# Output projection of a linear-attention layer as seven half products with features on the partitions

## The chip, the cores and the metric

One of the eight cores of a Trainium2 chip runs the whole program. The metric is the device time of one execution in microseconds. TensorE (PE) multiplies, VectorE (DVE), ScalarE (ACT) and GpSimd (POOL) work element by element, SyncE (SP) issues the loads and stores.

## What is computed

```python
qkv = silu(x @ qkv_w.T)                # 1024 tokens (4 batches of 256), 32 heads of 128 features
attn = linear_attention(q, k, v)       # decayed, causal, per head and batch
normed = norm_w * attn * rsqrt(mean(attn ** 2) + eps)    # over all 4096 features of a token
y = sigmoid(x @ gate_w.T) * normed
x = layernorm(x + y @ out_w.T)         # the output projection, 4096 -> 512
...                                    # then base projection, router, LoRA experts, a second layernorm
```

Everything is float32. Each factor of a product is split into a high part, rounded by the copy, and a low part, the rest, and a product takes three matmuls: high by high, high by low, low by high.

## The kernel before

The 32 heads are done in eight groups of four. The work of a group is a fixed order of stages, written out by hand for each engine; semaphores tie the queues together. The stages of group g are QK0 (q and k of the group's first head), V0 and V1 (the values of its four heads, half of the tokens each), the output stage for the group before, G01 (gates of two heads), QK1, G23, QK2, QK3. Attention and score matmuls of single heads stand between the products. The output stage of the last group is part of the tail.

**Projections in seven products.** A stage such as G01 multiplies a 2 by 2 arrangement of weight blocks by a 2 by 2 arrangement of token halves with seven products in place of eight (the Winograd form of Strassen's method). The sums of the token blocks are made once. Those of the weights are made per load: `sums` on GpSimd (L1737) makes four further blocks out of four loaded ones, in three instructions (L1742 with 512 columns, L1745 and L1749 with 256). ScalarE copies the high parts (`sums_hi`, L389), VectorE subtracts them for the low parts (`sums_lo`, L1031), in two parts: A has units 0 to 2, for products 1, 5 and 6, B has units 3 to 6, for products 2, 7, 3 and 4. The high and low parts live in a ring of 16 units. The full blocks are in two staging buffers, so that a load waits for the splits of the load two before it. TensorE runs p1, p4 of the stage before, p5, p6, p2, p7, p3 (L1976 and after); between them ScalarE copies banks (`u2_copy`, `p5_copy`, `u3_copy`) and VectorE adds (`c22_add`, `c12_add`), which p4 and the next stage's copies wait for.

**The output stage.** The weight rows of the four heads come in two loads, oa and ob (`rows_load`), and go to the ring as they are; ScalarE scales them by norm_w on the way (`out_rows_hi`, L407; `out_rows_lo`, L1052). The gated heads lie in `y`, features on the partitions. For each of eight tiles of 128 tokens ScalarE and VectorE split the four heads' columns (`y_split`, L548; `y_low`, L1138), TensorE multiplies with the y tile as the stationary operand, 4 heads by 3 terms of 512 columns (`output`, L1946), into banks 0 and 3 in turn, and VectorE adds the bank to `acc`, tokens on the partitions (`out_add`, L1142). The queues of all engines hold this work between that of V1 and G01: ScalarE's `output` (L711) and VectorE's `output` (L1280).

**GpSimd** has, in this order for a group: the sums of vb, four additions of squares (`add_squares`, L1756), the sums of g01, qk1, g23, and so on. **SyncE** issues loads in the order qk0, va, vb, decay, oa, ob, decay, g01, qk1, ...

**The scores.** For each batch five matmuls (`scores`, L1911); banks 4 to 7 hold scores and attention of the current head. The mask (`mask`, `mask_sum`) reads them on VectorE.

**The tail.** The last group's output runs tile by tile into eight banks (`tail_output`, L2166); VectorE scales by the inverse root mean square, adds x, and the layer norm, its transposes and the second half of the layer follow, in `acc`.

Of the kernel before, what the change touches and what calls it, by code (L numbers as in the profile page):

```python
# [47 lines left out]
SLOT = {"first_a": 0, "first_b": 4, "qk0": 0, "va": 7, "vb": 14, "oa": 5, "ob": 9, "g01": 13, "qk1": 4, "g23": 11, "qk2": 2, "qk3": 9}  # L48
# [10 lines left out]
DVE_X = 3  # L59

TAIL_BANK = [4, 5, 6, 7, 0, 1, 2, 3]

# [4 lines left out]
def load_no(g, name):  # L67

    if g == 0:
        return LOADS0.index(name)  # L70
    return len(LOADS0) + (g - 1) * len(LOADS) + LOADS.index(name)

# [20 lines left out]
def build(nc, stream, xt, x, decay, norm_w, base_b, lora_router, router_b, expert_map, ident_in, ones_in, fresh_in, out):  # L93
    ctx = ExitStack()
    with ctx:
# [23 lines left out]
        stg = sb("stg", [P, 4, W])  # L119
        first_out, c22_pre, c12_pre, p5s = stg[:, 0, :], stg[:, 1, :], stg[:, 2, :], stg[:, 3, :]  # L120
# [44 lines left out]
        yt = ((kh, kl), (qh, ql), (xh[:, 4, :], xl[:, 4, :]), (xh[:, 5, :], xl[:, 5, :]))  # L165
        quad = acc[:, :, :].rearrange("p t n -> p (t n)").rearrange("p (q n) -> p q n", q=4)
# [32 lines left out]
        y_done, y_hi, y_lo = sem("y_done"), sem("y_hi"), sem("y_lo")  # L199
# [7 lines left out]
        t_out = sem("t_out")  # L207
        ss_done, meansq_done, rms_done, power_set = sem("ss_done"), sem("meansq_done"), sem("rms_done"), sem("power_set")
        acc_scaled, last_added, x1_done, var_done = sem("acc_scaled"), sem("last_added"), sem("x1_done"), sem("var_done")
# [37 lines left out]
        def pieces(name, u0, u1):  # L247

            first = (SLOT[name] + u0) % RING
            n = u1 - u0  # L250
            if first + n <= RING:
                return [(first, 0, n)]
            return [(first, 0, RING - first), (0, RING - first, n - (RING - first))]

        def wait_free(eng, g, name, part):

            n = block_no(g, 0)
            if part == "A":
# [4 lines left out]
                elif name == "vb":  # L263
                    eng.wait_ge(p_done[4], n - NB + QK3 + 1)
                elif name == "oa":
                    eng.wait_ge(p_done[5], n + V1 + 1)
                elif name == "ob":
                    eng.wait_ge(p_done[3], n + V1 + 1)
                elif name == "g01" and g > 0:
                    eng.wait_ge(p_done[4], n + V1 + 1)  # L270
                elif name == "qk1":
                    if g > 0:
                        eng.wait_ge(o_done, TT * g)
                    else:
                        eng.wait_ge(d_done, 12)
# [6 lines left out]
            else:  # L282
                if name == "qk0":
                    eng.wait_ge(p_done[7], n - NB + QK2 + 1)
                elif name == "va":
                    eng.wait_ge(p_done[7], n - NB + QK3 + 1)
                elif name == "vb":
                    eng.wait_ge(p_done[7], n + QK0 + 1)
                elif name == "g01" and g == 0:
                    eng.wait_ge(d_done, 12)  # L290
# [8 lines left out]
        def _(sp):  # L299
            def block_load(m):  # L300

                s = m % 2
                if m >= 2:
                    sp.wait_ge(t_lo, 2 * (m - 2) + 2)
# [3 lines left out]
            def rows_load(m, n=2):  # L308

                s = m % 2  # L310
                if m >= 2:
                    sp.wait_ge(t_lo, 2 * (m - 2) + 2)
# [61 lines left out]
            for t in range(TT):  # L374
# [4 lines left out]
                sp.dma_start(out[tile(t), :], acc[:, t, :]).then_inc(stored[t], 16)  # L379
# [5 lines left out]
        def _(act):  # L385
# [3 lines left out]
            def sums_hi(g, name, part):  # L389

                m = load_no(g, name)
                act.wait_ge(t_sum, block_no(g, ["qk0", "va", "vb", "g01", "qk1", "g23", "qk2", "qk3"].index(name)) + 1)
                wait_free(act, g, name, part)
                u0, u1 = (0, 3) if part == "A" else (3, 7)
                runs = pieces(name, u0, u1)
# [11 lines left out]
            def out_rows_hi(g, name, e):  # L407
                wait_free(act, g, name, "A")
                if g == 1 and name == "oa" and e == 0:
                    act.wait_ge(const_in, 16 * (CONSTS - 1))  # L410
                rows_hi(load_no(g, name), SLOT[name] + 2 * e, e, HG * (g - 1) + 2 * (name == "ob") + e)

            def u2_copy(n):
                act.wait_ge(p_done[1], n + 1)
                act.wait_ge(c12_added, n)
                if n == 0:
                    act.wait_ge(d_out, 10)
                copy(ps[:, B1, :], ps[:, B0, :]).then_inc(cp01, 1)

            def p5_copy(n):  # L420
                act.wait_ge(p_done[5], n + 1)
                act.wait_ge(c12_added, n)
                act.wait_ge(c22_added, n)
                copy(p5s, ps[:, B5, :]).then_inc(cp5, 1)

            def u3_copy(n):
# [3 lines left out]
                if n == 0:  # L430
                    act.wait_ge(d_out, 11)
                copy(ps[:, B2, :], ps[:, B1, :]).then_inc(cp12, 1)
# [71 lines left out]
            def g11_out(n):  # L504
                act.wait_ge(p_done[2], n + 1)
                act.wait_ge(y_lo, TT * group_of(n))
# [41 lines left out]
            def y_split(g, t):  # L548

                act.wait_ge(y_done, 2 * HG * g - (2 if t < 4 else 0) + (1 if t < 4 else 0))  # L550
                if t >= 2:
                    act.wait_ge(o_done, TT * (g - 1) + t - 1)
                copy(yh[:, t % 2, :, :], y[:, :, tile(t)]).then_inc(y_hi, 1)
# [46 lines left out]
            def first_group():  # L600
# [10 lines left out]
                rows_hi(1, SLOT["first_a"], 0)  # L611
                rows_hi(1, SLOT["first_a"] + 2, 1)
# [3 lines left out]
                rows_hi(2, SLOT["first_b"], 0)  # L616
                rows_hi(2, SLOT["first_b"] + 2, 1)
# [29 lines left out]
            def qk0(g):  # L647
# [12 lines left out]
                square(h - 2, 1)  # L660
                q0_out(n, h)
# [4 lines left out]
            def v0(g):  # L666
                n, h = block_no(g, V0), HG * g
                u2_copy(n)
                if g > 0:
                    k0_out(n - 1, h)  # L670
                else:
                    k1_out(n - 1, h)
# [3 lines left out]
                if g > 0:  # L676
                    scores_hi(h - 1, 1)
                    part(h - 1, 0)
                v11_out(n)
                if g > 0:  # L680
                    square(h - 1, 0)
                v22_out(n)
                if g > 0:
                    y_split(g, 0)
                    y_split(g, 1)
                v12_out(n)

            def v1(g):
# [3 lines left out]
                if g > 0:  # L692
                    part(h - 1, 1)
                    square(h - 1, 1)
                p5_copy(n)
                if g > 0:
                    out_rows_hi(g, "oa", 0)
                u3_copy(n)
                if g > 0:
# [1697 lines left out]
```

## Time and profile before

| | before |
|---|---|
| median of 3 runs | 1015.74 us (1015.03 to 1015.87) |
| the profiled execution, its own time | 1015.99 us |
| its span, first to last instruction | 1014.2 us |
| TensorE, matmuls | 1000.2 us, 99% |
| VectorE | 780.2 us, 77% |
| ScalarE | 664.7 us, 66% |
| GpSimd | 350.0 us, 35% |

Busy time is the union of an engine's instructions. The duration of a matmul reaches from its start until its last column is out, and the next one starts before that; its price for the engine is the distance to the next start. The granted clock is the share of TensorE's full clock. In the timeline a line gives start, duration, engine, source line, operation, operands and shapes, and in brackets the idle time before it and what ended it.

### The profile page before, as it was taken

How to read it: one execution, taken by the hardware profiler on the slowest of the kernel's cores; microseconds unless marked ns; L12 is line 12 of the kernel's file. 1: busy time of each engine (PE TensorE's matmuls, PEld its weight loads, DVE VectorE, ACT ScalarE, POOL GpSimd, SP SyncE). 2: the span in 40 equal slices, each digit the busy share in tenths (PEclk: the TensorE clock that was granted, in tenths of full speed). 3: DMA queues.
4: the chain of work that ended last, by engine and by line, in shares of the span. 5: the costliest groups of instructions: out<-in, count | busy, mean ns of one | idle time of the engine just before them, and what ended most of it. 6: DMA issues, size and time to landing. Idle time of an engine off the chain costs nothing.

```text
span 1014.2 us, 15712 instructions
## 1 busy us (share of the span) xinstructions
PE 1000.2 (99%) x5620; PEld 874.8 (86%) x5620; DVE 780.2 (77%) x1102; ACT 664.7 (66%) x1108; POOL 350.0 (35%) x329
## 2 busy tenths in 40 slices
PE   9999999999999999999999999999999999999996
PEld 7888988889888898889988898888978899888886
DVE  6777975887857976779757879579777797699885
ACT  6577754777467764677647774677637786477644
POOL 1353232341443223433323414342234323331462
PEclk9999999999999999999999999999999999999999
DMA  6021111110211111211111112111112111110402
GB/s 202 27 63 51 50 47 55 56 47 28 68 42 47 48 55 41 62 48 53 47 56 55 39 35 68 42 47 48 47 48 63 35 65 48 42 48 22 146 22 83
DMA packets 48814, 55.67 MB, mean 55 GB/s; under 512 B 4321, under 2 KB 40033, under 8 KB 48737
## 3 DMA queue, kind: packets, MB, share of 16 engines
q1 hardware_dynamic: 48736, 54.67, 17.0%
q8 instruction: 45, 0.74, 0.3%
q14 instruction: 33, 0.26, 0.1%
HBM read 52.56 MB, written 2.10 MB: 54 GB/s over the span
## 4 chain that ended last, share of the span: by engine, by line
PE 87%; DVE 6%; issue 2%; ACT 2%; POOL 1%; DMA 1%; SPq 0%; POOLq 0%; DVEq 0%; ACTq 0%
PE ps L1833 20%; PE ps L1834 19%; PE ps L1835 19%; PE ps L1827 9%; PE ps L1828 8%; PE ps L1829 8%; PE ps L1940 1%; PE ps L1925 1%; DVE wl L1048 1%; PE ps L1942 1%; DVE s L1029 1%; PE ps L1927 1%; ACT wh L387 1%; DVE yl L1029 1%; DVE acc L1148 1%
## 5 line engine op out<-in xcount | busy, mean ns | idle before, releaser
L1833 PE MATMUL ps<-xh,wh 128*128 128x512 f32 x658 | 261.8, 398 | 0.6 <-ACT stg L435 0.6
L1834 PE MATMUL ps<-xl,wh 128*128 128x512 f32 x658 | 257.2, 391 | 0.0
L1835 PE MATMUL ps<-xh,wl 128*128 128x512 f32 x658 | 256.1, 389 | 0.0
L1742 POOL TENSOR_TENSOR stage<-stage 128x512 f32<-128x512 f32 x61 | 87.4, 1432 | 331.4 <-DMA stage<-stream 331.3
L1762 POOL TENSOR_TENSOR sqacc<-sqacc,sq 128x512 f32<-128x512 f32 x64 | 92.3, 1442 | 271.1 <-ACT sq L546 271.1
L1029 DVE TENSOR_TENSOR wl<-stage,wh 128x1024 fp32r<-128x1024 f32 (+2 forms) x145 | 159.4, 1109 | 32.1 <-ACT wh L387 32.1
L387 ACT ACTIVATE wh<-stage 128x1024 fp32r<-128x1024 f32 (+2 forms) x145 | 122.1, 855 | 53.8 <-PE ps L1829 33.7
L1835 PEld LDWEIGHTS ps<-xh,wl 128*128 128x128 f32 x658 | 123.6, 188 | 26.6
L1833 PEld LDWEIGHTS ps<-xh,wh 128*128 128x128 f32 x658 | 123.5, 188 | 24.0 <-issue 1.0
L1834 PEld LDWEIGHTS ps<-xl,wh 128*128 128x128 f32 x658 | 123.9, 188 | 22.0
L1833 PE MATMUL ps<-wh,xh 128*128 128x256 f32 (+1 forms) x416 | 121.1, 291 | 0.0
L1835 PE MATMUL ps<-wh,xl 128*128 128x256 f32 (+1 forms) x416 | 119.2, 287 | 0.0
L1834 PE MATMUL ps<-wl,xh 128*128 128x256 f32 (+1 forms) x416 | 119.0, 286 | 0.0
L387 ACT ACTIVATE ps<-ps 128x512 f32<-128x512 f32 x122 | 71.2, 584 | 33.6 <-PE ps L1835 33.2
L1827 PE MATMUL ps<-wh,yh 128*128 128x512 f32 x224 | 88.9, 397 | 1.3 <-DVE yl L1029 0.9
L1828 PE MATMUL ps<-wl,yh 128*128 128x512 f32 x224 | 87.4, 390 | 0.0
L1829 PE MATMUL ps<-wh,yl 128*128 128x512 f32 x224 | 87.3, 390 | 0.0
L1834 PEld LDWEIGHTS ps<-wl,xh 128*128 128x128 f32 x416 | 79.7, 192 | 0.3
L1833 PEld LDWEIGHTS ps<-wh,xh 128*128 128x128 f32 x416 | 79.3, 191 | 0.3
L1835 PEld LDWEIGHTS ps<-wh,xl 128*128 128x128 f32 x416 | 79.4, 191 | 0.0
L387 ACT ACTIVATE yh<-y 128x512 fp32r<-128x512 f32 x56 | 34.6, 631 | 66.2 <-PE ps L1829 66.2
L1029 DVE TENSOR_TENSOR s<-sfull,s 128x768 fp32r<-128x768 f32 x64 | 69.7, 1089 | 7.1 <-ACT s L387 5.9
(201 smaller groups left out, 2220.5 us busy)
## 6 DMA issues: line engine op xcount, KB each, us to landing
stage<-stream SPq DMA_DIRECT2D x61, 384.0 KB, 3.3
stage<-stream SPq DMA_DIRECT2D x42, 256.0 KB, 2.8
stage<-stream SPq DMA_DIRECT2D x63, 128.0 KB, 2.1
dec<-decay SPq DMA_DIRECT2D x32, 128.0 KB, 2.0
acc<-xt SPq DMA_DIRECT2D x8, 256.0 KB, 5.7
v<-x SPq DMA_DIRECT2D x8, 256.0 KB, 4.9
out<-acc SPq DMA_DIRECT2D x8, 256.0 KB, 2.1
sfull<-lora_router SPq DMA_DIRECT2D x1, 512.0 KB, 6.0
```

Of the source, the lines that this page charges most:

```text
L387: return nc.scalar.activation(dst, src, ACT.Copy, **kw)
L1029: return nc.vector.tensor_tensor(dst, full, f32(hi), ALU.subtract)
L1048: ins = nc.vector.scalar_tensor_tensor(out=lo, in0=full, scalar=nw[:, head:head + 1], in1=f32(hi), op0=ALU.mult, op1=ALU.subtract)
L1148: nc.vector.tensor_tensor(acc[:, t, :], acc[:, t, :], ps[:, B5 if t % 2 else B0, :], ALU.add)\
L1742: nc.gpsimd.tensor_tensor(stage[:, s, 1:5:3, :], stage[:, s, 0:6:5, :], stage[:, s, 7:8, :].broadcast_to([P, 2, U]), ALU.add).then_inc(t_p ...
L1762: nc.gpsimd.tensor_tensor(sqacc[:, e, :], sqacc[:, e, :], sq[:, :], ALU.add).then_inc(sq_added, 1)
L1827: nc.tensor.matmul(dst, wt[0], mv_[0], start=start, stop=False)
L1828: nc.tensor.matmul(dst, wt[0], mv_[1], start=False, stop=False)
L1829: return nc.tensor.matmul(dst, wt[1], mv_[0], start=False, stop=stop)
L1833: nc.tensor.matmul(dst, wt[0], mv_[0], start=start, stop=False, skip_group_check=True)
L1834: nc.tensor.matmul(dst, wt[0], mv_[1], start=False, stop=False, skip_group_check=True)
L1835: return nc.tensor.matmul(dst, wt[1], mv_[0], start=False, stop=stop, skip_group_check=True)
```

## The change

The output stage uses the seven-product form, too. oa and ob become blocks of a 2 by 2 arrangement (`out_block`): each holds two blocks of 128 output features for all four heads. They are loaded like other blocks, GpSimd scales them by norm_w in place (two instructions of 512 columns each) and makes their sums, and they are split in parts A and B. The weights are now the stationary operand, the y operands move in 512 columns, and each of the seven products is done for oa and for ob in turn: 14 groups of 6 matmuls, in banks 0 to 3 for oa and 4 to 7 for ob. The y operands are single blocks or sums of blocks, two heads by half of the tokens (1024 columns): four sums on GpSimd (`y_sums`), seven high copies on ScalarE (`operand_hi`) and seven low parts on VectorE (`operand_lo`). Two operands use the buffers of k and q, which are free after the scores of head h. Six bank copies on ScalarE and two additions of the fifth product on GpSimd (`p5_add`) are new; VectorE still adds eight banks, to `acc_t`, which has features on the partitions.

In the tail the sum is turned back: 32 transposes (`turned`) in eight fours go to banks, and VectorE scales them out of PSUM into `res` (`scaled`). Everything behind works in `res` and not in `acc`. The three first tiles' separate additions (`last_addition`) are gone. The ring places are computed for a period of 70 (`unit_slot`). The second part of va is split in QK0, later than before, behind vb's first part and `mask_sum`; some splits of g23 move. The matmuls of a score are in another order, with one start flag per bank.

```diff
-                    rows_load(load_no(g, "oa"))
-                    rows_load(load_no(g, "ob"))
+                    block_load(load_no(g, "oa"))
+                    block_load(load_no(g, "ob"))
...
+                if name in ("oa", "ob"):
...
+                    for units, head in ((slice(0, 8, 7), HG * (g - 1)), (slice(3, 6, 2), HG * (g - 1) + 2)):
+                        rows_ = stage[:, s, units, :].rearrange("p u (k n) -> p u k n", k=2)
+                        nc.gpsimd.tensor_tensor(rows_, rows_, nw[:, head:head + 2].unsqueeze(1).unsqueeze(3)
+                                                .broadcast_to([P, 2, 2, P]), ALU.mult).then_inc(t_part, 1)
...
+            def y_sums(g):
+
+                h = HG * g
+                a11, a12, a21, a22 = y_full[1], y_full[2], y_full[7], y_full[4]
+                pool.wait_ge(y_done, 2 * (h - 1) + 2)
+                pool.wait_ge(q1_lo, h + 1)
...
+                nc.gpsimd.tensor_tensor(y_temp, a21, a22, ALU.subtract).then_inc(y_sum, 1)
+                nc.gpsimd.tensor_tensor(a21, a21, a11, ALU.subtract).then_inc(y_sum, 1)
+                pool.wait_ge(y_sum, 4 * (g - 1) + 2)
+                pool.wait_ge(y_lo, operand_no(g, 1))
+                nc.gpsimd.tensor_tensor(a11, a11, y_temp, ALU.subtract).then_inc(y_sum, 1)
+                pool.wait_ge(y_sum, 4 * (g - 1) + 3)
+                pool.wait_ge(y_lo, operand_no(g, 5))
+                nc.gpsimd.tensor_tensor(y_temp, a12, a11, ALU.subtract).then_inc(y_sum, 1)
...
                     add_squares(h - 2, 0)
                     add_squares(h - 2, 1)
+                    sums(g, "oa")
                     add_squares(h - 1, 0)
+                    sums(g, "ob")
                     add_squares(h - 1, 1)
+                    y_sums(g)
+                    p5_add(g, 0)
+                    p5_add(g, 1)
                     sums(g, "g01")
```

VectorE's queue in V1 and the output stage, after the change:

```diff
             def v1(g):
                 n, h = block_no(g, V1), HG * g
+                add_part(h - 1, 1)
+                gated(h - 1, 1)
+                sums_lo(g, "oa", "A")
                 mask(h, 0)
+                mask_sum(h, 0)
                 c22_add(n)
-                mask_sum(h, 0)
+                sums_lo(g, "ob", "A")
                 c12_add(n)
...
                 scores_lo(h, 0)
+                operand_lo(g, 5)
                 mask(h, 1)
+                mask_sum(h, 1)
+                operand_lo(g, 6)
+                sums_lo(g, "oa", "B")

             def output(g):
                 h = HG * g
...
+                operand_lo(g, 2)
+                sums_lo(g, "ob", "B")
+                operand_lo(g, 7)
+                operand_lo(g, 3)
+                out_add(g, "c11", 0)
+                operand_lo(g, 4)
+                out_add(g, "c11", 1)
+                out_add(g, "c22", 0)
+                out_add(g, "c22", 1)
+                scores_lo(h, 1)
                 sums_lo(g, "g01", "A")
+                out_add(g, "c12", 0)
                 sums_lo(g, "g01", "B")
+                out_add(g, "c12", 1)
                 values_lo(h)
+                out_add(g, "c21", 0)
+                out_add(g, "c21", 1)
```

TensorE's output stage, and its tail:

```diff
+            def out_product(g, i, j, bank, start, stop):
+
+                slot = unit_slot(g, ("oa", "ob")[j], UNIT[i])
+                hi, lo = y_operand[i]
+                for k in range(2):
+                    last = mm3_onto(ps[:, bank + S_B * j, :], (wh[:, slot, tile(k)], wl[:, slot, tile(k)]),
+                                    (hi[:, k, :], lo[:, k, :]), start and k == 0, stop and k == 1)
+                last.then_inc(o_done, 1)
...
+                out_product(g, 1, 0, B0, True, False)
+                pe.wait_ge(s_parts, 2 * h + 1)
+                out_product(g, 1, 1, B0, True, False)
+                pe.wait_ge(y_lo, operand_no(g, 5))
+                pe.wait_ge(cp5, n + 1)
+                out_product(g, 5, 0, B5, True, True)
+                pe.wait_ge(s_parts, 2 * h + 2)
+                out_product(g, 5, 1, B5, True, True)
...
```

The products follow in the order 1, 5, 6, 2, 7, 3, 4, each waiting for its operand's low part.

```diff
-            for t in range(4):
+            for t in range(3):
+                turned(t)
+            tail_output(0, range(2, HG))
+            turned(3)
+            for t in range(1, 4):
                 tail_output(t, range(2, HG))
+            turned(4)
             tail_output(4, range(HG))
             transposed(0)
+            turned(5)
             tail_output(5, range(HG))
```

## Rows read from the trace of the kernel before

**Rows 1.** The page, parts 1 and 2: engines over the span, and granted clock.
```profile
PE 1000.2 (99%) x5620; PEld 874.8 (86%) x5620; DVE 780.2 (77%) x1102; ACT 664.7 (66%) x1108; POOL 350.0 (35%) x329
...
PEclk9999999999999999999999999999999999999999
```

**Rows 2.** Windows view: length, busy time (instructions) PE, PEld, DVE, ACT, POOL; clock; DMA.
```profile
482.00:497.00 15.00, 15.00 (x126) 14.96 (x125) 9.33 (x14) 9.81 (x18) 3.70 (x4) 1.00 0.12 36
497.00:519.00 22.00, 21.91 (x96) 17.54 (x96) 17.39 (x22) 7.68 (x11) 8.49 (x7) 1.00 0.18 54
```

**Rows 3.** Timeline of PE: first matmul of an output stage, first of G01.
```profile
496.60 0.40 PE L1827 MATMUL ps<-wh,yh 128*128 128x512 f32 x1
...
518.97 0.39 PE L1833 MATMUL ps<-xh,wh 128*128 128x512 f32 x1
```

**Rows 4.** Groups by line and form: one of the output stage's three matmul lines.
```profile
L1827 PE MATMUL ps<-wh,yh 128*128 128x512 f32 x224 | 88.9, 397 | 1.3 <-DVE yl L1029 0.9
```

**Rows 5.** Timeline of POOL, alone: start us, us, engine line operation.
```profile
430.02 1.30 POOL L1742 TENSOR_TENSOR stage<-stage 128x512 f32<-128x512 f32 x1 [7.46 <-DMA stage<-stream]
431.40 0.74 POOL L1745 TENSOR_TENSOR stage<-stage 128x256 f32<-128x256 f32 x1
```

**Rows 6.** Timelines of DVE and POOL over the same five microseconds.
```profile
457.06 1.50 DVE L1029 TENSOR_TENSOR s<-sfull,s 128x768 fp32r<-128x768 f32 x1
458.49 1.49 DVE L1029 TENSOR_TENSOR wl<-stage,wh 128x768 fp32r<-128x768 f32 x1
459.90 1.22 DVE L1029 TENSOR_TENSOR kl<-stg,kh 128x512 fp32r<-128x512 f32 x1
461.05 1.21 DVE L1029 TENSOR_TENSOR wl<-stage,wh 128x1024 fp32r<-128x1024 f32 x1
...
457.83 1.33 POOL L1745 TENSOR_TENSOR stage<-stage 128x256 f32<-128x256 f32 x1
459.24 1.33 POOL L1749 TENSOR_TENSOR stage<-stage 128x256 f32<-128x256 f32 x1
```

**Rows 7.** Timeline of DVE at the end of stage QK0.
```profile
469.50 0.41 DVE L1114 TENSOR_TENSOR sfull<-sfull 128x256 f32<-128x256 f32 x1
469.83 0.68 DVE L1073 TENSOR_TENSOR stg<-ps,stg 128x512 f32<-128x512 f32 x1
470.44 1.22 DVE L1029 TENSOR_TENSOR vl<-v,vh 128x1024 fp32r<-128x1024 f32 x1
471.57 0.95 DVE L1029 TENSOR_TENSOR s<-sfull,s 128x768 fp32r<-128x768 f32 x1
```

**Rows 8.** Timelines of SP and POOL: a block load and its first sum.
```profile
490.71 0.33 SPq L305 DMA_DIRECT2D stage<-stream  x1
491.08 0.44 SPq L306 DMA_DIRECT2D stage<-stream  x1
...
494.44 1.29 POOL L1742 TENSOR_TENSOR stage<-stage 128x512 f32<-128x512 f32 x1 [5.82 <-DMA stage<-stream]
```

**Rows 9.** Timeline of ACT in stage V1.
```profile
483.21 0.58 ACT L387 ACTIVATE ps<-ps 128x512 f32<-128x512 f32 x1
484.64 0.60 ACT L435 ACTIVATE v<-ps 128x512 f32<-128x512 f32 x1 [0.85 <-PE ps L1835]
...
497.56 1.06 ACT L387 ACTIVATE vh<-v 128x1024 fp32r<-128x1024 f32 x1 [0.16 <-ACT v L435]
498.52 0.83 ACT L387 ACTIVATE wh<-stage 128x768 fp32r<-128x768 f32 x1
```

**Rows 10.** Timeline of DVE: c22 of stage V0.
```profile
480.32 0.69 DVE L1064 TENSOR_TENSOR stg<-ps,stg 128x512 f32<-128x512 f32 x1 [1.39 <-PE ps L1835]
```

**Rows 11.** Timeline of PE in the tail, and its window there.
```profile
962.55 0.60 PE L2206 MATMUL ps<-ident,acc 128*128 128x128 f32 x4
962.90 0.49 PE L1827 MATMUL ps<-wh,kh 128*128 128x512 f32 x1
...
961.00:966.00 5.00, 5.00 (x27) 4.08 (x26) 4.32 (x7) 4.24 (x8) 2.22 (x6) 1.00 0.00 0
```

More of the change, by code:

```diff
@@ L71, in load_no, with unit_slot, part_no, splits_of_load @@
     return len(LOADS0) + (g - 1) * len(LOADS) + LOADS.index(name)
+def unit_slot(g, name, u):
+    if name in PAIRED:
+        a, b = PAIRED[name]
+        place = a + u if u < 3 else b + u - 3
+    else:
+        place = PLACE[name] + u
+    return (place + PERIOD * g) % RING
+def part_no(g, name, part):
+    m = load_no(g, name)
+    if name in ("va", "oa"):
+        return 2 * m + (1 if part == "A" else 3)
+    if name in ("vb", "ob"):
+        return 2 * m + (0 if part == "A" else 2)
+    return 2 * m + (1 if part == "A" else 2)
+def splits_of_load(m):
+    if len(LOADS0) <= m < TAIL_LOAD and LOADS[(m - len(LOADS0)) % len(LOADS)] in ("va", "oa"):
+        return 2 * m + 3
+    return 2 * m + 2
+def out_no(g, i, j):
+    return 14 * (g - 1) + 2 * OUT_ORDER.index(i) + j + 1
+def operand_no(g, i):
+    return 7 * (g - 1) + OUT_ORDER.index(i) + 1
 def block_no(g, place):
@@ L423, in p5_copy @@
                 act.wait_ge(c22_added, n)
+                if n > 0 and place_of(n) == G01:
+                    act.wait_ge(o_p5, 2 * group_of(n) - 1)
                 copy(p5s, ps[:, B5, :]).then_inc(cp5, 1)
@@ L1061, in c22_add @@
                 dve.wait_ge(k1_lo, heads_before(n))
+                if n > 0 and place_of(n) == G01:
+                    dve.wait_ge(o_p5, 2 * group_of(n))
                 if n == block_no(GROUPS - 1, QK3):
@@ L1843, in features, with values @@
                 return last
-            def values(i, bank, step, start, stop):
+            def values(g, i, bank, step, start, stop):
                 for t in range(2):
@@ L1861, in product @@
                 if b in (V0, V1):
-                    last = values(i, bank, b - V0, start, stop)
+                    last = values(group_of(n), i, bank, b - V0, start, stop)
                 else:
-                    last = features(i, bank, NAMES[b], start, stop)
+                    last = features(group_of(n), i, bank, NAMES[b], start, stop)
                 last.then_inc(p_done[i], 1)
@@ L2189, in tail_output, with turned @@
                     last.then_inc(t_out, 1)
+            def turned(t):
+                if t == 0:
+                    pe.wait_ge(o_added, TT * (GROUPS - 1))
+                    pe.wait_ge(c11_out, LAST + 1)
+                elif t == 1:
+                    pe.wait_ge(c12_added, LAST + 1)
+                elif t == 2:
+                    pe.wait_ge(c21_out, LAST + 1)
+                elif t == 3:
+                    pe.wait_ge(meansq_done, 1)
+                elif t < 7:
+                    pe.wait_ge(x1_done, t - 2)
+                else:
+                    pe.wait_ge(acc_scaled, 6)
+                for j in range(4):
+                    last = nc.tensor.transpose(ps[:, TURN_BANK[t], tile(j)], acc_t[:, j, tile(t)], ident[:, :])
+                last.then_inc(acc_turned, 1)
             def sum_of_squares():
@@ L2361 @@
             else:
-                hh = h - HG + 2 * (name == "ob")
-                blocks.append(rows(wo[hh], wo[hh + 1]))
+                blocks.append(out_block(h - HG, 2 * (name == "ob")))
     wb = np.asarray(L0_ffn_base_W).reshape(HID, KT, P).transpose(1, 2, 0)
```

490 lines of the change are left out of this document (268 added, 222 removed).

## The prediction

> **What bounds the kernel now.** I read the page first. TensorE is busy for 1000.2 of 1014.2 us, at full granted clock [rows 1], so the first question is what the change does to TensorE's work, and the second whether the other engines can still feed it. The mean durations of its matmuls mislead here: 397 ns each [rows 4], but they overlap. The timeline gives the pace: the 96 matmuls of an output stage begin at 496.60 and the next stage begins at 518.97 [rows 3], 22.37 us or 0.233 us each. The stage table then shows who has room: in the 22 us of that output stage VectorE is busy 17.39 us, in the 15 us before it (stage V1) 9.33, and GpSimd 8.49 and 3.70 [rows 2].
>
> Last I read VectorE and GpSimd side by side, because the change gives both more to do in these stages. Alone, GpSimd takes 1.30 us for 512 columns and 0.74 for 256 [rows 5]. Beside a VectorE instruction with two SBUF operands, 256 columns take 1.33, and VectorE's 768 columns take 1.50 where 0.95 is usual [rows 6, 7]. In rows 6 the two take strict turns: the 256-column sum that starts at 459.24 ends at 460.57, the VectorE instruction queued at 459.90 ends its 512 columns 0.48 us after that, where the next one starts (461.05). The VectorE instruction of 768 columns that could go when GpSimd was done at 459.16 gave way to the next by 459.94. So a turn costs 0.6 to 0.64 us for GpSimd at 256 columns, 0.5 for VectorE at 512 and 0.78 at 768; scaled from those and from the lone durations, 1.2 for GpSimd at 512 and 1.05 for VectorE at 1024. VectorE instructions that read PSUM take no turn.
>
> **TensorE's saving.** Seven products for two halves, two tiles and three terms are 84 matmuls of 512 columns in place of 96 ([rows 4]: 224 of each of three kinds in 7 stages). 12 x 0.233 = 2.8 us a group, 19.6 us over seven. The score matmuls only change order: 0.
>
> **The tail.** 32 transposes are added, in eight fours. A four costs 0.35 us, plus 0.08 of slower restart in the matmul behind it [rows 11]: 8 x 0.43 = 3.4 us. TensorE has no idle time there (5.00 of 5.00), so it is all on the path. Below that 0 if some gaps hide them, above it 6 if a transpose waits for a bank. Three VectorE additions become three scalings of about the same length: 0.
>
> **What feeds the output stage.** Per group ScalarE trades eight copies of 512 and four scaled ones for seven of 1024, four of the weight blocks and six PSUM copies, about 7 us more; it has the room. A 1024-column copy costs 0.96 from start to start, recorded as 1.06 [rows 9]. VectorE gets seven operand differences of 1024 at 1.13 [rows 7] for eight of 512 at 0.60, and four block differences of 768 and 1024 for four of 512: about 5 us more. GpSimd gets most: sums for oa and ob (each two scalings of 512, one sum of 512, two of 256), four sums of y at 1024 columns, two additions of P5 at 1024.
>
> No row has GpSimd at 1024 columns. Bounds: 1.3 us, if width were free, and 2.6, twice the 512 row. The step from 256 to 512 adds 0.56, so two more steps give 1.30 + 1.1 = 2.4, and 2.3 as a turn; I take this. The Trainium skill (GPSIMD Engine Reference, Elementwise: side-by-side cycle accounting) gives some 2.6 cycles per element for such an instruction and 4497 ns for 2048; by it an estimate of 2.3 us, hardly another sum.
>
> **When GpSimd can start.** The load of oa waits for the second part of va, whose split moves in the queue behind the mask sum of stage QK0. That sum ends at 469.83 [rows 7]; with 1.14 for the split, 470.97. A block load is in use 3.7 us after its first issue (490.71 to 494.44, [rows 8]): GpSimd starts oa at 474.8 (until now that load was asked for right behind va's split at the start of QK0; behind it in SyncE's queue stand ob and a decay table that only stage G23 reads) and from there has work in one queue up to the sums of g01, without which VectorE cannot prepare g01 and TensorE cannot start stage G01.
>
> **The sum of turns, from 474.8 to the start of G01.** GpSimd: nine of 512 (10.8), six of 256 (3.8), six of 1024 (13.8), 28.4 us. VectorE, two SBUF operands only: four q and k differences (2.0), three mask sums (0.8), six of 768 (4.7), nine of 1024 (9.45), 16.9 us. Together 45.3: G01 no earlier than 520.1 if the turn is never left unused. Without any stall TensorE would be there at 518.97 - 2.8 = 516.2. Before it was 518.97. [...]
>
> Step by step, with PSUM instructions and waits put in, the turns are not always used. V1's first product is copied at 483.21 and p4 is out at 484.64 [rows 9], so V1 starts near 481.7 at 1.43 a product. The stretch of q and k differences in V0 now alternates with oa, so that c22 of V0, at 480.32 today [rows 10], is written by 483.75: p4 in V1 starts 0.6 late. GpSimd ends the sums of ob at 492.3 and the last squares at 493.7. Then: difference a21-a22 to 496.3; VectorE's split of ob to 497.0; a21-a11 to 499.3; scores to 500.1; third sum to 502.4; operand 5 to 503.45. TensorE did product 1 twice from 497.35 to 500.15 and stands until 503.5. The mask and its sum, delayed by the fourth y sum, put operand 6 at 507.3 (product 5 ended 506.3). Then four VectorE splits of 1024 (oa, operand 2, ob, operand 7) alternate with the two P5 additions: product 2 in its second half starts at 513.0, product 7 at 516.35, product 3 at 519.15, product 4 at 521.95, end 524.75. The g01 split is done at 524.5. So G01 starts at 524.75 and not at 518.97: **+5.8 us a group**, made of -2.8 of matmuls and 8.6 of stalls. Seven groups: +40.5. Where a stall at operand 5 went away, operand 6 and the P5 additions are late next, as the turns stay the same; that is why I trust the sum more than its places. In G01 the queue behind is a few us long, but p2 and p7 come 4 to 5 us later: 0.
>
> The profiled execution took 1015.99 us, 1.8 beyond its span and 0.25 above the median of 1015.74, so no correction. 1015.99 + 40.5 + 3.4 = **1060 us**. About 0.2% (2 us) is what a measurement of this kernel can tell from no change.
>
> **The rivals.**
> - **The feed holds** (0.16), faster. Place: operands 5 and 6 and g01's split reach TensorE in time; price -19.6 + 3.4: 999.8 us. For it: TensorE leads each operand by two products, VectorE and GpSimd are idle for parts of every stage [rows 2]. Against: the turn sum. It decides at G01 starting before 518.5; my steps would have to shrink by 6.2 us, about what six wide GpSimd instructions give at the lower bound of 1.3 us instead of 2.3.
> - **Near balance** (0.07): part of it, 2.3 us of stalls a group, cancels the saving: 1016 to 1020.
> - **Turns packed tighter** (0.19): the stalls overlap better, G01 at 521.5 to 522.5, +3 a group: 1015.99 + 21 + 3.4 = 1040 us. For it: the bound of 520.1 leaves room below my 524.75.
> - **The delay spreads** (0.08): backlog reaches p7 of G01 or QK1, or V0 loses more: +8 a group, 1075 us.
> - The forecast itself has 0.50.
>
> **How the numbers follow.** 1060 is the likeliest case, itself good for 1048 to 1069 with the wide GpSimd instruction between 2.0 and 2.6. The range goes down to the tighter packing and below, and up to the spread: 1018 to 1076. That leaves out the fast rival (0.16) and some 0.05 at the two ends. Faster 0.16, within 0.2% 0.04, slower 0.80.
>
> **What would show it.** TensorE's matmul count falls by 252 of 512 columns and gains 32 transposes, while its idle time rises from 14 us to some 60. The waits list shows TensorE behind VectorE's operand and block splits, worst at products 5, 6, 2 and 7. GpSimd's 1024-column y sums take 2.4 us or more, and its busy time rises from 350 to about 550. VectorE's mean for two-SBUF instructions rises, while out additions stay near 0.68. V1's start to G01's start grows from 37.2 us to some 43. Wrong would be: output stages of 19.6 us with no waits inside, or wide GpSimd instructions near 1.3 us. If V0 or QK0 show the stalls instead, the place of the late queue was wrong and not the turn.

## The result, and the profile after

| | before | after |
|---|---|---|
| median | 1015.81 us (4 runs, 1015.03 to 1015.93) | 1062.07 us (4 runs, 1061.72 to 1062.58) |
| the profiled execution's span | 1014.2 us | 1059.9 us |
| TensorE idle in the span | 14.0 us | 62.9 us |
| output stage, its start to G01's, mean of seven | 22.43 us | 25.85 us |
| G01 to the next output stage, mean of six | 96.38 us | 98.64 us |

The ratio is 1.0457, with an interval of [1.0439, 1.0476]: 4.6% slower. First the page of the kernel after, parts 1 and 2; it answers to [rows 1].

```profile
PE 997.0 (94%) x5568; PEld 860.6 (81%) x5568; DVE 902.3 (85%) x1105; ACT 704.1 (66%) x1153; POOL 565.4 (53%) x441
...
PEclk9999999999999999999999999999999999999998
```

TensorE has less to do and stands more: its span less its busy time rose by 48.9 us. The granted clock is full up to the last slice, as before, so what was lost is idle time. The window view of the kernel after shows where, in stage V1 and in the output stage of the group of [rows 2]; its columns are the same.

```profile
501.00:516.00 15.00, 14.35 (x119) 14.00 (x117) 12.06 (x13) 9.80 (x16) 14.48 (x10) 1.00 0.00 1
516.00:542.00 26.00, 20.05 (x82) 14.95 (x83) 25.97 (x21) 15.59 (x21) 20.27 (x10) 1.00 0.14 46
```

VectorE is busy for 25.97 of 26 us, where it was busy for 17.39 of 22, and GpSimd for 14.48 of V1's 15 us, where it was 3.70. Neither is simply full: a VectorE instruction counts as busy while it stands for GpSimd. The timeline of TensorE after, those lines of this output stage that have idle time in front of them:

```profile
516.13 0.50 PE L1956 MATMUL ps<-yh,wh 128*128 128x512 f32 x1 [0.78 <-DVE wl L1129]
520.34 0.50 PE L1956 MATMUL ps<-kh,wh 128*128 128x512 f32 x1 [1.16 <-DVE kl L1129]
524.33 0.50 PE L1956 MATMUL ps<-q,wh 128*128 128x512 f32 x1 [0.94 <-DVE q L1129]
528.90 0.47 PE L1956 MATMUL ps<-yh,wh 128*128 128x512 f32 x1 [1.55 <-DVE yl L1240]
532.13 0.50 PE L1956 MATMUL ps<-yh,wh 128*128 128x512 f32 x1 [1.61 <-DVE wl L1129]
534.36 0.50 PE L1956 MATMUL ps<-kh,wh 128*128 128x512 f32 x1 [0.57 <-DVE kl L1129]
```

These are products 1, 5, 6, 2, the half of product 2 for ob, and 7; G01 starts at 542.65. What each waited for ended just before, and the timelines of the kernel after over the same time, VectorE's lines first and GpSimd's below them, say why it was late:

```profile
513.52 2.55 DVE L1129 TENSOR_TENSOR wl<-stage,wh 128x768 fp32r<-128x768 f32 x1
...
516.60 2.55 DVE L1129 TENSOR_TENSOR s<-sfull,s 128x768 fp32r<-128x768 f32 x1
519.08 1.21 DVE L1129 TENSOR_TENSOR kl<-stg,kh 128x1024 fp32r<-128x1024 f32 x1
...
525.34 3.42 DVE L1240 SCALAR_TENSOR_TENSOR yl<-y,yh 128x1024 fp32r<-128x1024 f32 x1
528.68 3.40 DVE L1129 TENSOR_TENSOR wl<-stage,wh 128x1024 fp32r<-128x1024 f32 x1
...
510.31 2.40 POOL L1851 TENSOR_TENSOR stg<-y 128x1024 f32<-128x1024 f32 x1
512.68 2.58 POOL L1852 TENSOR_TENSOR y<-y 128x1024 f32<-128x1024 f32 x1
515.34 3.00 POOL L1855 TENSOR_TENSOR y<-y,stg 128x1024 f32<-128x1024 f32 x1
520.43 2.43 POOL L1858 TENSOR_TENSOR stg<-y 128x1024 f32<-128x1024 f32 x1 [2.10 <-DVE kl L1129]
525.28 5.71 POOL L1868 TENSOR_TENSOR acc<-acc,stg 128x1024 f32<-128x1024 f32 x2 [2.42 <-ACT stg L448]
530.96 2.26 POOL L1833 TENSOR_TENSOR stage<-stage 128x512 f32<-128x512 f32 x1
```

The first y sum does not stand for VectorE: 2.40 us for 1024 columns. The third ends at 518.34, and the VectorE instruction queued at 516.60, 768 columns and 0.95 us when alone, ends at 519.15: it stood until the sum was done and took 0.81 us from there. The split of ob at 513.52, of the same size, stood behind the second sum. The two additions of P5 take 5.71 us as a pair; beside them two VectorE instructions of 1024 columns, 1.21 us each when alone, take 3.42 and 3.40.

Where the 45.7 us between the spans lie, by the starts of the stages: 3.9 ahead of the first output stage, 24.0 in the seven output stages (3.42 each), 13.6 in the six stretches between them (2.27 each: 1.3 of it in V1, the rest in G01 and QK1), 4.3 behind the last. Of the 3.9, 3.0 are one wait for ob's part A ahead of the first output stage, in front of 144.48; that stage is in turn the shortest of the seven (23.8 us).

### The profile page after: what moved, and what is told of

It is laid out like the page before. It is cut to its first block, busy times and chain, and to the rows that moved or that the text cites. A ratio compares the mean times of both kernels' runs of the same rounds, so it can differ in the third digit from the quotient of the medians.

```text
span 1059.9 us, 15875 instructions
## 1 busy us (share of the span) xinstructions
PE 997.0 (94%) x5568; PEld 860.6 (81%) x5568; DVE 902.3 (85%) x1105; ACT 704.1 (66%) x1153; POOL 565.4 (53%) x441
## 4 chain that ended last, share of the span: by engine, by line
PE 71%; DVE 17%; issue 5%; ACT 2%; POOL 2%; DMA 2%; SPq 0%; DVEq 0%; POOLq 0%; ACTq 0%
PE ps L1956 18%; PE ps L1957 17%; PE ps L1958 17%; DVE wl L1129 5%; PE ps L1950 3%; PE ps L1952 3%; PE ps L1951 3%; DVE kl L1129 3%; PE ps L2053 2%; DVE s L1129 2%; DMA stage<-stream 2%; DVE yl L1240 1%; PE ps L2047 1%; PE ps L2049 1%; PE ps L2048 1%
## 5 line engine op out<-in xcount | busy, mean ns | idle before, releaser
L1129 DVE TENSOR_TENSOR wl<-stage,wh 128x768 fp32r<-128x768 f32 (+3 forms) x183 | 222.0, 1230 | 35.6 <-ACT wh L448 35.6
L1833 POOL TENSOR_TENSOR stage<-stage 128x512 f32<-128x512 f32 x75 | 116.6, 1555 | 208.6 <-DMA stage<-stream 207.3
L448 ACT ACTIVATE wh<-stage 128x768 fp32r<-128x768 f32 (+3 forms) x183 | 148.2, 834 | 47.3 <-POOL stage L1840 37.6
L448 ACT ACTIVATE ps<-ps 128x512 f32<-128x512 f32 x150 | 87.4, 583 | 43.5 <-PE ps L1958 42.3
L1840 POOL TENSOR_TENSOR stage<-stage 128x256 f32<-128x256 f32 x75 | 88.1, 1175 | 5.9
L1836 POOL TENSOR_TENSOR stage<-stage 128x256 f32<-128x256 f32 x75 | 79.6, 1062 | 5.9
L1129 DVE TENSOR_TENSOR s<-sfull,s 128x768 fp32r<-128x768 f32 x64 | 75.4, 1178 | 5.5 <-ACT s L448 5.2
L1129 DVE TENSOR_TENSOR kl<-stg,kh 128x512 fp32r<-128x512 f32 (+1 forms) x71 | 71.8, 1014 | 3.0 <-ACT stg L496 2.9
L448 ACT ACTIVATE s<-sfull 128x768 fp32r<-128x768 f32 x64 | 53.8, 841 | 27.1 <-DVE sfull L1211 26.9
```

The costliest lines, as they stand in the source:

```text
L448: return nc.scalar.activation(dst, src, ACT.Copy, **kw)
L1129: return nc.vector.tensor_tensor(dst, full, f32(hi), ALU.subtract)
L1833: nc.gpsimd.tensor_tensor(stage[:, s, 1:5:3, :], stage[:, s, 0:6:5, :], stage[:, s, 7:8, :].broadcast_to([P, 2, U]), ALU.add).then_inc(t_p ...
L1836: nc.gpsimd.tensor_tensor(stage[:, s, 2, :], stage[:, s, 1, :], stage[:, s, 5, :], ALU.add)\
L1840: nc.gpsimd.tensor_tensor(stage[:, s, 6, :], stage[:, s, 2, :], stage[:, s, 3, :], ALU.add)\
```

## The experiments

Each kernel has a difference to the kernel before on the same chip; after minus before is 46.3 us, and "back" is what of that a kernel gives back. In the first two sets both kernels ran once on a chip, and single runs of before lay between 1014.2 and 1018.3 us over the chips, so a difference is good to some 2 us, and 4 us are possible.

Three theories. **Turns**: VectorE instructions with two SBUF operands and GpSimd instructions that read SBUF go strictly one at a time, and the sum of their turns is the stall. **Queue**: GpSimd's list has become too long, whatever it does beside VectorE. **VectorE**: its own added work is the limit.

**no_scaling**: GpSimd's four scalings by norm_w are left out.

```diff
-                    for units, head in ((slice(0, 8, 7), HG * (g - 1)), (slice(3, 6, 2), HG * (g - 1) + 2)):
...
-                        nc.gpsimd.tensor_tensor(rows_, rows_, nw[:, head:head + 2].unsqueeze(1).unsqueeze(3)
-                                                .broadcast_to([P, 2, 2, P]), ALU.mult).then_inc(t_part, 1)
```

> The changed kernel without the scaling of the weight blocks by norm_w on GpSimd (28 instructions of 512 columns; the weights stay unscaled). Three theories. Turns: VectorE's instructions with two SBUF operands and GpSimd's hold one path in turn, and that sets the output stage; four turns of 1.2 us less a group, mostly early, give some 4 us a group, so about 1032 us. Queue: GpSimd's own list of work is what is late, whatever it reads; 5.2 us shorter a group, also about 1030. VectorE: its own 5 us of new work a group is the bound; no change, 1060 to 1062.

Measured: 1047.01 against 1017.11, 16.4 us back. That is 2.3 us for each group, about half of what turns and queue said. In its fifth output stage the granted clock stood at 0.50 for some 3 us, and that stage took 25.6 us where the others took 22.5 to 24.2, so about 1.7 us of the time are not the scaling's.

**small_y_sums**: the four y sums cut from 1024 to 8 columns, operands 5 and 3 taken from single blocks; the values of the sums are left out.

```diff
-                nc.gpsimd.tensor_tensor(y_temp, a21, a22, ALU.subtract).then_inc(y_sum, 1)
+                nc.gpsimd.tensor_tensor(y_temp[:, :, 0:4], a21[:, :, 0:4], a22[:, :, 0:4], ALU.subtract).then_inc(y_sum, 1)
...
```

> The changed kernel with the four y sums of a group cut from 1024 columns to 8 each (the operands of products 5 and 3 are unsummed blocks, so these sums are left out of the computation). Turns: 9 us of turns a group are gone, nearly all stalls of the output stage with them, 1003 to 1012 us. Queue: the same. VectorE: 1055 to 1062, since its own work is unchanged.

Measured: 1020.58, 42.8 us back, nearly all of it, though 9 to 18 us less than forecast. The output stages shrink to 20.8 us on average. The stretches between them stay at 97.5 to 99.1, where they were 96.4: the first sign that over 1 us a group is not in the output stage.

**write_only_y_sums**: each y sum replaced by GpSimd fills of about the same length (1024, 1024 and 512 columns), which read nothing; the sums are left out.

```diff
+            def fill(dst):
+                link(nc.gpsimd.memset(dst, 0.5))
+                link(nc.gpsimd.memset(dst, 0.5))
+                nc.gpsimd.memset(dst[:, 0:1, :], 0.5).then_inc(y_sum, 1)
...
-                nc.gpsimd.tensor_tensor(y_temp, a21, a22, ALU.subtract).then_inc(y_sum, 1)
+                fill(y_temp)
...
```

> The four y sums of a group are replaced by fills of the same destinations, three in a row, together as long as a sum (about 2.4 us), so that GpSimd is as busy but reads nothing from SBUF; the sums are left out of the computation. Turns: VectorE no longer stands behind them, 1.5 to 2 us of stalls are left a group: 1012 to 1024 us. Queue: GpSimd's list is as long as before, so 1058 to 1062. VectorE: 1058 to 1062.

Measured: 1038.67, 24.7 us back, between the two forecasts. The timelines of this kernel in V1, VectorE's lines and below them GpSimd's:

```profile
502.07 0.95 DVE L1129 TENSOR_TENSOR wl<-stage,wh 128x768 fp32r<-128x768 f32 x1
502.94 0.69 DVE L1170 TENSOR_TENSOR stg<-ps,stg 128x512 f32<-128x512 f32 x1
503.59 0.96 DVE L1129 TENSOR_TENSOR s<-sfull,s 128x768 fp32r<-128x768 f32 x1
...
501.35 0.96 POOL L1845 MEMSET stg<- 128x1024 f32 x1
502.36 0.53 POOL L1846 MEMSET stg<- 128x512 f32 x1
502.83 0.95 POOL L1844 MEMSET y<- 128x1024 f32 x1
503.84 0.96 POOL L1845 MEMSET y<- 128x1024 f32 x1
```

The same VectorE instruction, the split of ob's part A, takes 0.95 us beside fills and took 2.55 at 513.52 beside a sum. So contention it is, and by reading. Of the 42.8 us that the sums cost, 24.7 come back when they no longer read; the other 18.1 are put down to their time in GpSimd's queue, ahead of the P5 additions and of g01's sums. The Trainium skill (SBUF: State Buffer, Who interferes with whom) says the same of the first part: a VectorE instruction with two SBUF inputs contends with a GpSimd instruction that reads SBUF, not with one that only writes it. The rows agree, with 2.55 and 0.95 us.

**small_p5_adds**: the two additions of P5 cut to 8 columns, so that P5 is missing from the sums.

```diff
-                nc.gpsimd.tensor_tensor(dst, dst, p5_home[j]..., ALU.add).then_inc(o_p5, 1)
+                nc.gpsimd.tensor_tensor(dst[:, :, 0:4], dst[:, :, 0:4], ..., ALU.add).then_inc(o_p5, 1)
```

> The two additions of the fifth product to the sum of y on GpSimd are cut from 1024 to 8 columns (the rest is left out of the computation). Turns: 4.6 us of turns fewer a group, but late in the stage; the stalls before products 5 and 6 (about 1.2 and 1.0 us) stay and those at product 2 and later shrink: about 3 us a group, near 1041 us. Queue: the same or more, 1035 to 1041. VectorE: 1060.

Measured: 1032.07, 31.3 us back, 4.5 a group; 9 us more than turns forecast, and 3 more than queue. The output stage is 21.9 us in all groups but the first; the stalls before products 1, 5 and 6 remain, those behind are gone. 16.4 + 42.8 + 31.3 is nearly twice the loss: these are not separate prices, but cuts in one queue whose last entry, g01's split, starts G01. The theory of VectorE's own work fell four times.

The next runs move work instead of leaving it out. **act_scale**: ScalarE scales in place, eight copies of 256 columns a group.

```diff
+                        copy(rows_, rows_, scale=nw[:, head + k:head + k + 1]).then_inc(o_scaled, 1)
```

> The scaling of oa's and ob's blocks by norm_w moves from GpSimd (four instructions of 512 columns a group) to ScalarE (eight in-place copies of 256 columns, placed where V0's and V1's banks are already out); everything is computed. If leaving the scaling out gained its 15 us by freeing turns and GpSimd's queue, ScalarE has the room and the same comes back: 1045 to 1050 us, TensorE waiting for 'kl' and 'wl' as with the scaling left out. If ScalarE had itself become tight (it is busy 66% now and 9.8 of 15 us in V1), the copies delay the bank copies in front of V1's p4 or GpSimd's sums: 1055 us or more.

Measured: 1048.16 against 1017.06, 15.2 us back, as forecast and as when it was left out. Here, too, the clock stood at 0.50 in the fifth output stage, for some 7 us, and that stage took 26.7 us where the others took 23.2 to 24.2.

**p5_on_vector**: VectorE adds P5 from its bank.

```diff
-                nc.gpsimd.tensor_tensor(dst, dst, p5_home[j]..., ALU.add)...
+                nc.vector.tensor_tensor(dst, dst, ps[:, B5 + S_B * j, :]..., ALU.add)...
```

> P5 is added to c12 and c21 by VectorE straight from its bank; ScalarE's two copies of P5 and GpSimd's two wide additions go. Everything is computed. Theory 'turns': two GpSimd instructions of 2.4 us alone (5.7 us as two records with their turns) leave, two VectorE instructions of 1024 columns with one PSUM operand, about 1.2 us each, come and take no turn: most of the 30 us of the cut additions stays, 1035 to 1045 us. Theory 'VectorE's time': it gets 2.4 us a group more in a stage in which it is busy for 25.97 of 26 us: 1055 to 1065 us.

Measured: 1038.87, 24.4 us back, as turns said. The fullest engine got 2.4 us a group more to do, and the kernel became faster. The groups by line of this kernel have the fourteen new instructions, with their mean:

```profile
L1268 DVE TENSOR_TENSOR acc<-acc,ps 128x1024 f32<-128x1024 f32 x14 | 16.9, 1208 | 0.0
```

1.21 us each is what 1024 columns take alone: an instruction with one operand in PSUM takes no turn.

**both_moved** has the two edits together.

> Scaling on ScalarE and P5 on VectorE together; GpSimd keeps only the block sums and the y sums of the new work; everything is computed. If the two places where TensorE waits are separate (the scaling decides when V0 and operand 1 to 5 are ready, P5 when the later splits are), the gains add: 1020 to 1030 us. If both gains are the same wait at the end of one queue (g01's split), they overlap: 1033 to 1045 us. If the feed were then wide enough for all of the products, 1002 us.

Measured: 1022.14, 41.2 us back; the two gains add (39.6), as the first forecast had it. The output stage is 20.7 us on average, but the rest of the group still 98.8.

**one_turn_of_four** prices the tail's transposes.

```diff
-                for j in range(4):
+                for j in range(1):
```

> In the tail only one of the four transposes of each of the eight tiles is done (24 of 32 left out, the rest of the bank is read as it is). By the prediction's price (0.35 us of a four and the restart) this takes off 24/32 of 3.4, some 2.5 us: 1059.5. By the comparison of the two tails (1.75 us longer from the last group's squares to the end) it takes off at most 1.3 us, 1060.8, and if the transposes lie in gaps of TensorE's that stay, nothing.

Measured: 1061.79, 1.5 us back, less than one run can tell. By its trace, from the last G01's start to the end, it takes 140.8 us, after took 142.6 and before 138.3: 1.8 us for 24 transposes, between the two forecasts. All 32 would be 2.4. The total can't show it: this run had the clock at 0.50 for some 7 us behind 144 and 3 us behind 659.

Then the order. In the trace of both_moved TensorE stood 0.9 us for ob's part A, 1.0 for operand 6, and 1.2 in QK1. **order_only** and **moved_v1_order** change V1's order, the first (with QK1's too) on the kernel after, the second on both_moved; **moved_both_orders** adds QK1's. In all three TensorE's first product no longer waits for ob's part A. ScalarE makes operand 6's high part one place earlier, and in QK1 VectorE does `gated` ahead of the split of qk2. The edit in VectorE's V1 and in ScalarE's QK1:

```diff
-                c12_add(n)
-                scores_lo(h, 0)
                 operand_lo(g, 5)
+                c12_add(n)
+                scores_lo(h, 0)
                 mask(h, 1)
...
-                sums_hi(g, "qk2", "A")
                 square(h, 0)
                 u3_copy(n)
+                sums_hi(g, "qk2", "A")
```

> Only the order of the queues differs from the changed kernel, no instruction is added or left out: TensorE's first product for oa waits for oa's part A alone, VectorE splits operand 5 ahead of c12 and of the scores, ScalarE copies operand 6 ahead of v12, and in QK1 the split of qk2's part A stands behind the square of the first half. Theory 'turns' (the work of the two engines that take turns is the limit, its places are not): the stalls move to other waits, under 2 us a group come back, 1050 to 1060 us. Rival 'order' (the hand-written order is what makes operands 5 and 6 late, the work would fit): 3 us or more a group, 1040 us or less.

Measured: 1066.24 against 1016.5: 3.5 us slower than after, outside both forecasts. The output stages grew to 28.2 us and the stretches between them fell to 97.4.

> The kernel with the scaling on ScalarE and P5 on VectorE, and the order in V1 and the output stage changed as described for the run on order alone; QK1 as before. In its trace TensorE stood 0.9 us for ob's part A and 1.0 for operand 6 in each group: with both gone, 1.3 to 1.9 us a group, 1009 to 1013 us. If the turns only move, under 0.5 us a group, 1019 us or more.

Measured: 1032.38, 10.8 us slower than both_moved by the differences to before, where 9 to 13 faster was forecast.

> The same with QK1's order changed as well, all of the computation in it. TensorE lost 1.2 us a group in QK1 to ScalarE's queue (the split of qk2's part A waited there for GpSimd's sums, ahead of the square and of the copies that free the banks). With that gone too a group takes some 116.8 us against 118.74 before the change: 1003 to 1007 us, faster than both kernels by 1% and 5%. If that wait comes back at another copy: 1010 to 1014 us.

Measured: 1026.60, ratio to before 1.0101 [1.0084, 1.0118], outside both forecasts. TensorE in it loses most in front of product 5's half for ob. Its timeline has the first line here; below stand VectorE's lines just ahead of it, and GpSimd's:

```profile
505.04 0.79 PE L1971 MATMUL ps<-kh,wh 128*128 128x512 f32 x1 [2.44 <-DVE sfull L1217]
...
500.83 2.83 DVE L1141 TENSOR_TENSOR s<-sfull,s 128x768 fp32r<-128x768 f32 x1
503.69 0.69 DVE L1215 TENSOR_TENSOR sfull<-ps,dec 128x512 f32<-128x512 f32 x1
504.30 0.68 DVE L1217 TENSOR_TENSOR sfull<-ps,dec 128x512 f32<-128x512 f32 x1
...
500.45 2.40 POOL L1875 TENSOR_TENSOR stg<-y 128x1024 f32<-128x1024 f32 x1 [2.09 <-DVE kl L1141]
```

The fourth y sum waits for operand 5; with that made earlier the sum was earlier too, and took the turn in front of the scores' split. Behind the split stands the mask, and it frees the banks of the product. A 1.3 us saving became a 2.4 us stall, since I moved the release of GpSimd's sum without asking what would stand at its turn. The turn is not all of it: the mask ends 2.9 us later than in both_moved (504.98 for 502.14, with product 1 at 498.33 and 498.39), and 1.1 of that is operand 5's own split, now ahead of it, 1.9 the turn. And the stall has a second price. The window behind it, with the columns of [rows 2]:

```profile
505.00:508.50 3.50, 3.46 (x9) 2.74 (x10) 3.48 (x4) 1.36 (x2) 0.00 (x0) 0.53 0.00 0
```

The granted clock fell to the lower level, 1.2 GHz, and matmuls of 512 columns start every 0.43 us instead of 0.23. So it is in five of the seven output stages, which take 23.3 to 23.5 us; in the third and the sixth the clock stays full, and they take 22.5 and 22.6. That is 0.9 us each time, over 4 of the 10 us by which this kernel is slower than before. The other half of the edit did what it should: with QK1's order the stretch between output stages is 96.4 to 96.9 us, that of before, in five of six. (The last has 98.6, from one wait of 1.9 us in V1 that both_moved has as well and that stays unexplained.) The timeline of ScalarE in both_moved, stage QK1, shows what the loss had been:

```profile
534.17 0.85 ACT L448 ACTIVATE wh<-stage 128x768 fp32r<-128x768 f32 x1 [1.17 <-POOL stage L1857]
534.92 0.58 ACT L619 ACTIVATE sq<-ps 128x512 f32<-128x512 f32 x1
535.40 0.59 ACT L448 ACTIVATE ps<-ps 128x512 f32<-128x512 f32 x1
537.25 0.39 ACT L448 ACTIVATE sq<-ps 128x256 f32<-128x256 f32 x1 [1.26 <-POOL sqacc L1897]
```

qk2's copy waits for GpSimd's late sums; the square behind it in ScalarE's queue is late, so GpSimd's addition of squares is, and for that the next part waits, ahead of the copies that free TensorE's banks.

**moved_sum_early** was meant to use all of this. In it `y_first_sum` makes a21 - a11 in V0:

```diff
+                    y_first_sum(g)
                     sums(g, "ob")
-                    add_squares(h - 1, 1)
                     y_sums(g)
                     sums(g, "g01")
+                    pool.wait_ge(t_lo, part_no(g, "g01", "B"))
+                    add_squares(h - 1, 1)
                 sums(g, "qk1")
```

> VectorE's and ScalarE's order in V1 is put back. To the kernel with the scaling on ScalarE and P5 on VectorE it adds: QK1's new order; the sum a21 - a11 made first, in V0, where GpSimd stands, with operand 6 then a22 less that sum and operand 3 in a21's place; the fourth addition of squares moved behind g01's split; and TensorE's first product waiting for oa's part A alone. All of the computation is in it. Theory 'turns': a wide sum and a 512-column instruction leave the unbroken alternation between 489 and 501 us, operands 5 and 6 are in time, the output stage takes 19.8 to 20.4 us and the rest of the group 96.5: 1000 to 1007 us, 1 to 1.6% faster than before the change. If the 0.9 us for operand 6 stays and only QK1's 1.2 us comes back: 1011 to 1015 us. If a waiting VectorE instruction again stands behind a wide sum ahead of a mask, as in the runs on the order: over 1017 us.

Measured: 1055.97, ratio 1.0392 [1.0376, 1.0407]. The output stages are what was forecast, 20.1 to 20.4 us. But the rest of a group is 103.3 to 105.9, so the time lies over 1017 us without the third forecast's mechanism. TensorE's list of waits (us in total, times, longest) has one large line; below it stand two windows around one of these waits, with the columns of [rows 2], and two lines of GpSimd's timeline, behind g01's split:

```profile
PE ps L1978 <- ACT ps L448: 31.8, 7, 4.9
...
536.00:541.00 5.00, 1.60 (x8) 0.98 (x6) 3.51 (x4) 0.00 (x0) 4.84 (x4) 1.00 0.34 105
541.00:549.00 8.00, 6.54 (x17) 5.16 (x18) 2.48 (x2) 3.96 (x6) 4.63 (x5) 0.57 0.23 68
...
535.94 1.29 POOL L1902 TENSOR_TENSOR sqacc<-sqacc,sq 128x512 f32<-128x512 f32 x1 [5.95 <-DVE wl L1141]
537.19 2.25 POOL L1850 TENSOR_TENSOR stage<-stage 128x512 f32<-128x512 f32 x1
```

The wait that I added, to keep the squares out of VectorE's way, held GpSimd for 5.95 us, and qk1's sums stood behind it. ScalarE waited for those with the first bank copy of G01 behind, and TensorE stood 4.9 us for that copy. Behind each of the seven waits the granted clock fell to 0.50 for some 3 to 7 us. Counted from G01's start against the kernel before, TensorE is 5.0 us late at the matmul that waited (3.9 in the last group), and in the first six groups the slow matmuls behind it add another 1.4 to 2.9 us. So 5 us of the 7 to 8 that a group lost are the wait, and over 2 the clock. With the squares behind qk1's sums an estimate from its output stages (20.2) and the rest of moved_both_orders (96.6) would be 116.8 us a group against 118.8 before. That was not tried, and no kernel here beats the one before: both_moved, the best with all of the computation, is 5 us (0.5%) slower on one run each.

## Why the prediction was right

It said 1060.0 us and slower; measured 1062.07. By its own steps:

- **Turns, and the price of a wide GpSimd instruction**: right, 2.4 alone, 2.40 measured. GpSimd busy 565.4 (some 550 foreseen), TensorE idle 62.9 (some 60).
- **The sum of its rows**: sound. 12 matmuls fewer a group are 84 in seven; the 252 among its signs is a slip, and the page shows 5568 for 5620, that is 84 fewer and 32 transposes more. No other sum used 252.
- **The places**: right in order and nearly in size, with products 5 and 6 two us earlier than forecast. Counted from the start of product 1, products 5, 6, the second half of 2, and 7 were put at 6.2, 10.0, 15.7 and 19.0, G01 at 27.4 us; they came at 4.2, 8.2, 16.0, 18.2 and 26.5. Product 1 itself came later than the step had it: 1.3 us a group were lost in V1 where 0.75 was foreseen (497.35 for 496.60), since the first product waits for the splits of both oa and ob, and the one of ob stood behind a y sum (0.78 us in front of 516.13).
- **The sum over turns, 45.3 us, as a bound**: it held. From GpSimd's first scaling of oa to G01 it took 50.20 us in this group (492.45 to 542.65) and 49.1 to 50.6 in all seven; the step by step forecast was 49.95. write_only_y_sums shows that the reading matters. What the argument missed is that turns are not the whole: of what the y sums cost, 18 of 43 us stay when they read nothing. The sum counted them rightly, as GpSimd's work in one queue, but the prediction told it as contention.
- **"In G01 the queue behind is a few us long, but p2 and p7 come 4 to 5 us later: 0"**: this step failed. About 1.0 us a group was lost in G01 and QK1, by the chain through ScalarE's queue that moved_both_orders undoes. The time is lost at the end of G01 and in QK1, and nothing behind that up to V1. I had asked only whether g01's own splits would be in time, not what stood in ScalarE's queue behind a copy that waits for GpSimd.
- **+5.8 us a group**: 5.63 measured from output stage to output stage (3.42 in the output stage, 1.3 in V1, 0.9 behind). The total is nearer than its parts, and in that it was lucky: the output stage was put at 5.0 and gave 1.6 less, V1 gave 0.5 more, and the step that failed made up the rest. Over seven groups 11 us too much met 10 us too little.
- **The tail, 3.4 us**: too high. 2.4 by one_turn_of_four's trace. 2.3 of the 4.3 us behind the last G01's start are lost in the first 21 us, far ahead of the transposes, and the forecast has nothing there: most of it is one wait for ScalarE (1.29 us in front of 929.47). moved_both_orders, with both moves and QK1's order, still has it (1.34 us), so these edits do not touch its cause, which stays open.
- **The rivals**: the feed did not hold; both_moved shows how far off it was, since with GpSimd busy for 88.6 us less than after (476.8) the time is still above before. "Turns packed tighter" and "delay spreads" both had a part of the truth that cancelled.

## What to carry to other kernels

Before work goes to GpSimd beside a VectorE that subtracts SBUF from SBUF, add up the turns of both engines, from when GpSimd can start to what TensorE needs last; busy shares of 35% and 77% hid a sum of 45.3 us where the kernel before had 44.2 (474.8 to 518.97). Work on an operand in PSUM, or on ScalarE, takes no turn: here two moves gave back 41 of 46 us. And every wait, added or moved, is judged by what is queued behind it on its engine: twice in this study a correct idea for one stall made a larger one there, and in most places TensorE's clock fell behind the new stall, so that it cost more than its length.

## What the runs showed that was not expected

- A turn of GpSimd's may cost VectorE a whole wide instruction: 768 columns took 0.95 us beside fills, 2.55 behind a y sum, 2.83 at worst for the scores' split in moved_both_orders. An instruction of 256 columns on VectorE (L1211) went from 472 ns on average to 890.
- GpSimd's fill of 1024 columns takes 0.95 us, its sum of 1024 takes 2.40: an instruction that only writes costs less than half.
- Order alone, without one instruction more, moved a group by over a microsecond either way: QK1's gave back 1.2 us in the stretch between output stages (97.8 to 96.6, medians of six), V1's made the output stage of both_moved 23.0 us on average where it was 20.7.
- A stall of TensorE's can cost its clock as well: 4.9 us of standing were followed by 3 to 7 us at 0.50 in every group of moved_sum_early. It need not show in the time. order_only has the clock at 0.50 in six places, and of its output stages the second, without such a place, takes 28.1 us, the third, with 7 us of it, 27.8, and the fifth, with as much, 30.8.
